# Three front attention layers taken by four streams in one round instead of two streams in two rounds

## The reference

```python
x = L0(x, ctx)   # Q = x@Wq+bq; K = ctx@Wk+bk; V = ctx@Wv+bv; x + softmax(Q K^T / 16) V @ Wo + bo
x = L1(x, ctx)   # the same Q, K, V; softmax over the QUERY axis; layernorm(x + w @ V) * gamma + beta
x = L2(x, ctx)   # as L0, with its own weights
for l in range(6):                                        # the decoder, 16 heads of 64
    tn = ln(t);  t = mha(tn, tn, ..., self_mask) + t
    tn = ln(t);  t = mha(ctx, tn, ..., ctx_mask) + t
    tn = ln(t);  t = t + relu(tn @ w1 + b1) @ w2 + b2
```

## Time and profile before

| | |
|---|---|
| median of 3 runs | 2991.25 us (2989.89 to 2992.86) |
| the profiled execution | 2991.18 us |
| its span, first to last instruction | 2989.4 us |
| TensorE matmul busy | 2846.2 us (95%) |
| VectorE, ScalarE, GpSimd busy | 1680.7, 1302.6, 963.4 us |
| mean granted TensorE clock | 0.991 |
| first matmul of the decoder | 247.99 us after the start |

### The profile page before, as it was taken

The page is one execution under the profiler, slowest core; times in us unless marked ns, Lnnn a source line. Parts: engine busy times, 40 slices in busy tenths (PEclk is TensorE's granted clock), DMA queues, the critical chain, the costliest instruction groups (busy, mean ns, idle before and its releaser), DMA issues.

```text
span 2989.4 us, 69468 instructions
## 1 busy us (share of the span) xinstructions
PE 2846.2 (95%) x23656; PEld 2311.2 (77%) x23656; DVE 1680.7 (56%) x6361; ACT 1302.6 (44%) x4274; POOL 963.4 (32%) x1169
## 2 busy tenths in 40 slices
PE   6677999999999999999999999999999999999999
PEld 4455878878878878878878878878878878878877
DVE  2344655655655655655655655655655655655655
ACT  2123444444444444444444444444444444444444
POOL 0101333333333333333333333333333333333333
PEclk9899999999999999999999999999999999999999
DMA  5003011033011032011033011032011032011010
GB/s 161 27 0 84 2 28 29 1 88 76 26 28 29 1 88 74 28 28 29 2 88 73 29 28 29 2 88 74 28 28 29 1 88 72 30 28 29 1 29 14
DMA packets 132257, 120.64 MB, mean 40 GB/s; under 512 B 15261, under 2 KB 121318, under 8 KB 130278
## 3 DMA queue, kind: packets, MB, share of 16 engines
q1 hardware_dynamic: 131942, 116.53, 15.5%
HBM read 115.59 MB, written 0.92 MB: 39 GB/s over the span
## 4 chain that ended last, share of the span: by engine, by line
issue 48%; POOL 25%; PE 21%; DVE 2%; ACT 1%; POOLq 1%; DMA 0%; SPq 0%; DVEq 0%; ACTq 0%
POOL prob L541 18%; PE proj L581 8%; PE proj L601 3%; POOL prob L511 3%; PE sum L601 3%; PE sum L769 2%; POOL ctx_parts L532 1%; PE proj L573 1%; POOL tw L491 1%; PE score L745 1%; PE tr L756 1%; DVE qcT L1197 1%; POOLq L540 1%; POOL ctx_parts L529 1%; POOL rstd L488 1%
## 5 line engine op out<-in xcount | busy, mean ns | idle before, releaser
L541 POOL TENSOR_TENSOR prob<-prob,rtotal 128x375 f32<-128x375 f32 x672 | 543.4, 812 | 762.4 <-DVE rtotal L1465 761.4
L964 ACT ACTIVATE prob<-prob,negmax 128x375 f32<-128x375 f32 (+1 forms) x688 | 418.8, 609 | 453.6 <-DVE negmax L1456 423.2
L887 PE MATMUL sum<-pT,ctx 32*128 32x224 f32 (+1 forms) x4608 | 500.6, 358 | 12.6 <-DVE qcT L1448 12.6
L887 PE MATMUL tr<-pT,ctx 32*128 32x224 f32 (+1 forms) x4608 | 500.6, 358 | 0.0
L887 PEld LDWEIGHTS sum<-pT,ctx 32*128 32x128 f32 (+1 forms) x4608 | 417.7, 185 | 73.2 <-issue 73.2
L1456 DVE CUSTOM_DVE_ANT_0 prob<-score,cbias 128x375 f32<-128x375 f32 x672 | 358.5, 533 | 195.0 <-PE score L581 193.6
L887 PEld LDWEIGHTS tr<-pT,ctx 32*128 32x128 f32 (+1 forms) x4608 | 417.0, 185 | 0.0
L581 PE MATMUL score<-ctx_parts,qc_high 128*128 128x376 f32 x1344 | 411.8, 387 | 0.0
L1474 DVE STREAM_TRANSPOSE pT<-prob 128x384 f32<-128x384 f32 x672 | 374.3, 560 | 0.0
L511 POOL TENSOR_TENSOR prob<-prob,rtotal 112x448 f32<-112x448 f32 x200 | 186.6, 933 | 543.7 <-DVE rtotal L1324 543.7
L1035 ACT ACTIVATE prob<-prob,negmax 112x112 f32<-112x112 f32 x800 | 298.9, 377 | 85.1 <-DVE negmax L1342 85.1
(11 more groups left out here) (170 smaller groups left out, 4763.2 us busy)
## 6 DMA issues: line engine op xcount, KB each, us to landing
ctx<-ctx SPq DMA_DIRECT2D x192, 176.0 KB
w_kv<-sa_kv SPq DMA_DIRECT2D x6, 2048.0 KB, 10.1
f<-ff_w SPq DMA_DIRECT2D x12, 1024.0 KB, 7.9
cmask<-ctx_mask SPq DMA_DIRECT2D x24, 375.0 KB, 4.7
w_q<-sa_q SPq DMA_DIRECT2D x6, 1024.0 KB, 11.3
w_o<-sa_ow SPq DMA_DIRECT2D x6, 1024.0 KB, 5.7
c_q<-ca_q SPq DMA_DIRECT2D x6, 1024.0 KB, 8.4
c_o<-ca_ow SPq DMA_DIRECT2D x6, 1024.0 KB, 10.8
```

What stands on the lines that cost most here:

```text
L541: pool.tensor_tensor(row, row, rtotal[:, G * SG + i:G * SG + i + 1].broadcast_to([P, S2]), ALU.mult).then_inc(prob_ready, 1)
L887: ins = pe.matmul(bank[:, 0:HT * R], ctx4[keys_of, m // (HALVES // NB), j, :], pT[keys_of, m % 2, :, j * R:(j + 1) * R], start=j == 0, sto ...
L964: act.activation(o, i, ACT.Exp, bias=negmax[0:rows, col:col + 1], scale=scale, accum_out=total[0:rows, col:col + 1]).then_inc(exp_ready, 1)
```

## The change

The front takes all four pairs in one round (`NU = PAIRS`), so its loop and the loads between rounds are gone. The order stays, with more streams in it: query and keys of stream 0, then for each stream the next query, its own scores, the next keys. The transpositions at a layer's head alternate between `proj0` and `sum0`. In the middle layer VectorE normalises stream u-1 right after the statistics of stream u. The buffers of streams 2 and 3 lie in `c_q`, `w_o`, `kT`, `before_low` and `f_1`; the context rows lie in `ctx4`, the masks in `c_o` and in the second half of `pT`, where the eighth buffer of probabilities is too. As `w_o` is borrowed, its load moves behind the front. The context masks get a semaphore of their own and are loaded later, with the self mask, behind the front's weights. Per pair, each engine has the same arithmetic instructions as before.

```diff
-    NU = 2
-    ROUNDS = PAIRS // NU
+    NU = PAIRS
+    FRONT_TR = ("proj0", "sum0")
...
+        own = (v_all, f2_flat, cq_flat, wo_flat)
+        fkT = [a[:, 0:k_end].rearrange("p (b k n) -> p b k n", b=NB, k=EK) for a in own]
+        faT = [tnT_next] + [by_chunk(kT_flat[:, u * EK * T2:(u + 1) * EK * T2]) for u in range(NU - 1)]
+        fprob = [prob_flat[:, m * S2B:(m + 1) * S2B] for m in range(NB * NU - 1)] + [pT_rest[:, 2 * NB * S2:2 * NB * S2 + S2B]]
...
 SyncE
             for u in range(NU):
-                load_pair_x(u, u)
-            load_pair_smask(0)
+                load_pair_x(u)
...
+            load_pair_smask(0)
+            for u in range(NU):
+                load_pair_fmask(u)
             load_qkv(0)
-            load_w_o(0)
             load_ca(0)
...
-            with sp.Fori(1, ROUNDS) as i:
-                for u in range(NU):
-                    sp.wait_ge(front_done, (i - 1) * NU + u + 1)
-                    load_pair_x(i * NU + u, u)
-                    load_pair_ctx(i * NU + u, u)
             sp.wait_ge(front_done, PAIRS)
+            load_w_o(0)
             load_c_q_o(0)
...
 TensorE
-            with pe.Fori(0, ROUNDS) as i:
-                pe.wait_ge(x_loaded, (i + 1) * (32 * NU))
+            pe.wait_ge(x_loaded, 16 * NU)
...
-                        transposes_of(at, ftw[u])
-                    pe.wait_ge(taken["proj0"], at.emptied("proj0", at.n["proj0"]))
+                    transposes_of(at, ftw[u], FRONT_TR[u % 2])
+                turned_to = {name: at.n[name] - NU // 2 for name in FRONT_TR}
+                def front_query(u):
+                    name = FRONT_TR[u % 2]
+                    pe.wait_ge(taken[name], at.emptied(name, turned_to[name] + u // 2 + 1))
...
-                    front_query(1)
-                    front_scores(0)
-                    front_keys(1)
-                    front_scores(1)
+                for u in range(NU):
+                    if u + 1 < NU:
+                        front_query(u + 1)
+                    front_scores(u)
+                    if u + 1 < NU:
+                        front_keys(u + 1)
...
 VectorE
+                for u in range(NU):
+                    if u + 1 < NU:
+                        front_query(u + 1)
+                    front_maxima(u)
+                    if u + 1 < NU:
+                        front_keys(u + 1)
+                    front_probabilities(u)
...
                         statistics(at, ftw[u], u)
+                        if u > 0:
+                            front_normalise(u - 1)
+                if n == 1:
+                    front_normalise(NU - 1)
             for u in range(NU):
...
+                if u == 0:
+                    dve.wait_ge(fmask_loaded, 16 * NU)
```

More of the change, by code:

```diff
@@ L257, in attention_layers @@
[L257 to L263, removed]
@@ L494, in _ @@
             pool.wait_ge(rows_loaded, 16 * ROW_DMAS)
[L495 to L504, removed]
+            at = Place(FRONT_LOOP)
+            for u in range(NU):
+                name = FRONT_TR[u % 2]
+                pool.wait_ge(ready[name], at.at(name, u // 2 + 1))
+                add_bias(fbias[0:S, 0, :], ftw[u])
+            for u in range(NU):
+                inverse_std(at, 1, u)
+            for u in range(NU):
+                name = FRONT_TR[u % 2]
+                before = {"proj0": 9 * NU - NU, "sum0": 2 * NU + NU}[name]
+                pool.wait_ge(ready[name], at.at(name, before + u // 2 + 1))
+                add_bias(fbias[0:S, 1, :], ftw[u])
             def normalise_group(at, g):
@@ L703, in _ @@
-                    if n != 1:
-                        for u in range(NU):
-                            pe.wait_ge(taken["proj0"], at.emptied("proj0", before["proj0"] + u + 1))
-                            out_rows(at, [faT[u][:, e, :] for e in range(EK)], [fwo[n][:, e, :] for e in range(EK)])
-                at.check()
+                            name = f"tr{b}"
+                            pe.wait_ge(prob_ready, at.at("prob", (n * NU + u) * NB + b + 1))
+                            bank = fill(at, name)
@@ new lines, in _ @@
+                            for j in range(KJ):
+                                ins = pe.transpose(bank[0:KR, j * S:(j + 1) * S],
+                                                   fprob[NB * u + b][0:S, j * KR:(j + 1) * KR], ident[0:S, 0:S])
+                            done(ins, name)
+                if n == 0:
+                    pe.wait_ge(ctx_loaded, 16 * NU)
+                if n == 1:
+                    pe.wait_ge(rows_loaded, 16 * ROW_DMAS)
+                for u in range(NU):
+                    for b in range(NB):
+                        if n != 1:
+                            pe.wait_ge(taken[f"tr{b}"], at.emptied(f"tr{b}", before.get(f"tr{b}", 0) + u + 1))
+                        else:
+                            pe.wait_ge(prob_ready, at.at("prob", (n * NU + u) * NB + b + 1))
+                        project(at, f"sum{b}", [fctxN[u][:, b, j, :] for j in range(KJ)],
+                                [probT[:, b, j, u * S:(u + 1) * S] for j in range(KJ)])
@@ new lines, in _ @@
+                for u in range(NU):
+                    for b in range(NB):
+                        pe.wait_ge(taken[f"sum{b}"], at.emptied(f"sum{b}", before.get(f"sum{b}", 0) + u + 1))
+                    if n != 1:
+                        for e in range(EK):
+                            project(at, f"proj{e}", [fwv[n][:, e * P:(e + 1) * P]], [fcT[u][:, :]])
+                    else:
+                        bank = fill(at, "proj1")
+                        for b in range(NB):
+                            o = bank[0:S, b * E:(b + 1) * E]
+                            pe.matmul(o, fcT[u][:, b * S:(b + 1) * S], fwv[n], start=True, stop=False)
+                            for j in range(KJ):
+                                ins = pe.matmul(o, probT[:, b, j, u * S:(u + 1) * S], fbias[0:KR, 2, :], start=False,
+                                                stop=j == KJ - 1)
+                        done(ins, "proj1")
@@ L709, in _ @@
+                if n != 1:
+                    for u in range(NU):
+                        pe.wait_ge(taken["proj0"], at.emptied("proj0", before["proj0"] + u + 1))
+                        out_rows(at, [faT[u][:, e, :] for e in range(EK)], [fwo[n][:, e, :] for e in range(EK)])
+            at.check()
             pe.wait_ge(front_done, PAIRS)
```

428 lines of the change are left out of this document (202 added, 226 removed).

## The result

The changed kernel takes 2963.88 us (median of 4 runs, 2962.96 to 2966.03) against 2992.06 (4 runs, 2989.89 to 2993.15): a ratio of 0.9907, 95% interval 0.9895 to 0.9919. That is 28.2 us less, where 31.8 was forecast; the time lies 0.6 us inside the upper end of the stated range (2964.5). Its profiled execution, whose rows follow, took 2966.03 us with a span of 2964.20 and was the slowest of the four: against the profiled execution before (2991.18) it is 25.2 us less.

A forecast was written before the change was run, and what follows sets the result against it. Only the first 247.99 us, the front, could gain; the decoder's 2741.41 us stay. Start 15.0, layers 63.6, 69.4 and 59.6, end 8.55 sum to 216.2: 31.8 us less, 2959.4, range 2955.5 to 2964.5 (chance 0.66).

The forecast's parts named there:

- (a): Layer one's head: four transpositions alternating two banks need not wait for ScalarE's copy, 4.0 us.
- (b): Layer one: the opening query, key and query fills ahead of the first scores, at the low clock, 9.03 us.
- (c): Layer one: four streams' scores, with a period of 8.0 us where a query comes between, 24.7 us.
- (d): Layer one: end of last scores to first sums, 3.35 us plus 0.95 per further stream, 5.25 us.
- (e): Layer one: first sums to first output, each further stream adding 1.35 us of sums and about 1.1 of value projection, 10.2.
- (f): Layer one: four outputs, each waiting for VectorE to empty the one bank, 2.83 us apart, 10.44 us.
- the seam: Layer two's last residual add to layer three's query: two streams still normalised, GpSimd meetings adding 1.2 us, 9.9 us.
- end of the front: Before the decoder: four pairs instead of two stored and masked behind the last add, 8.55 us, a loss of 2.35.
- (1): Rival: TensorE's clock does not fall between layers two and three; 3.0 us less, 2956.5; chance 0.12.
- (2): Rival: inserted streams in the front have a period of about 9.5 us; 9 more, 2968.5; chance 0.14.
- (3): Rival: late output weights hold the decoder's first pass, slower only beyond 83 us after request; chance 0.03 with its like.
- (4): Rival: longer load queue replaces the gap, TensorE waits 8 us or more for layer one's context rows; 2967 to 2972; 0.04.

The follow-up runs named there:

- the repeated run: The changed kernel run again without edits, beside three of the edited kernels: 2963.14 us, ratio 0.9901.
- The first experiment: The changed kernel with extra matmuls, results unread, where TensorE waits among the probability transpositions of layers one and three: 2957.06 us, ratio 0.9887.
- fillers alone: The changed kernel with unread extra matmuls at the start, in the tails, in the middle seam and before the decoder, no other edit: 2952.32 us, ratio 0.9871.
- transpositions inside: The changed kernel with each stream's probability transpositions and copies put behind the next stream's scores: 2953.67 us, ratio 0.9875.
- three edits: The changed kernel with probability transpositions behind the next stream's scores, the third layer's bias adds late and stores early: 2946.78 us, ratio 0.9853.

## Why the prediction was right, and where it was off

The mechanism was right: the gap between the rounds and the second start from cold are gone, the periods are as forecast and the decoder stays. The size is 28.2 of 31.8 us by the medians, and part of that fit is luck. In the profiled execution the decoder's first matmul comes 7.8 us later than forecast (6.1 in the profile of the repeated run, 222.29) and the gain is 25.2 us; the forecast's terms for the outer layers were too small. By its steps, in the profiled execution:

| step | forecast | measured |
|---|---|---|
| first transposition | 15.0 | 14.95 |
| layer one: transpositions (a) | 4.0 | 4.73 |
| opening (b) | 9.03 | 8.18 |
| four scores (c) | 24.7 | 24.45 |
| last scores to first sums (d) | 5.25 | 6.67 |
| first sums to first output (e) | 10.2 | 12.96 |
| four outputs (f) | 10.44 | 10.65 |
| layer two | 69.4 | 70.14 |
| of it the seam | 9.9 | 10.30 |
| layer three | 59.6 | 62.59 |
| of it the opening | 9.03 | 7.96 |
| of it last scores to first sums | 5.25 | 6.22 |
| of it sums to output | 10.2 | 13.31 |
| end of the front | 8.55 | 8.64 |
| first matmul of the decoder | 216.2 | 223.96 |
| decoder | 2741.4 | 2740.24 |

**The terms that were off** are (d) and (e), in both outer layers. In (e) I doubled the 2.70 us of 24 sums, taken at full clock, and applied the low clock only behind the holes that I had listed. The tail of transpositions doubled too, and behind it the clock fell: 2.4 and 2.8 us of the 2.8 and 3.1 that (e) misses. The first experiment gave them back. The rest of (e) is a value projection that turns in 1.25 us (67.82, 69.07), not 1.1. In (d) I read a turn as 0.93 us from the distance of two transpositions into different banks; what recurs is the turn of one bank, 1.25 us (55.51, 56.76). 3.35 + 2 x 1.25 makes 5.85, and with the clock kept the tail of layer three takes 5.83 and that of layer one 6.25, where VectorE stands 0.5 us ahead of its last division for no reason that the profile shows. The low clock adds 0.4 in each. The pieces of the turn were in the trace of before: a transposition of 0.55 (159.84), its copy of 0.51 (160.43) and 0.14 from a copy's end to the next transposition (159.70 to 159.84). I took a distance for a period.

**What held only in sum** is (a) with (b): ScalarE loads a table of 1.28 us (16.03) ahead of its first copy, so two banks do not make four transpositions back to back, and (a) is 0.7 longer; 0.85 us came back in the opening. The start's 14.95 fits 15.0, but the other kernels with the same loads have 13.7 to 14.1, so that fit is partly chance.

**Rivals.** (1) The clock kept in the seam: no; a transposition took 1.01 and the opening 7.96 us. With fillers alone it was kept, and they took 0.60 and 6.37: so this is worth 2.0 us and not 3.0. (2) Longer periods: no, 7.93 and 8.55 (91.68 to 100.23), as forecast. (3) Late output weights: the decoder changed by 1.2 us, downwards. (4) Waits for context rows: none; the chain runs from 17.93 on without a load. The four context requests did hold SyncE's queue, for 13.82 us instead of 7.99, and this was hidden as forecast.

**Two terms of the second layer.** The seam's forecast of 9.9 holds 2.3 us for meetings with GpSimd (1.2, and 1.1 within the 9.44 of before); taking them away gave 2.7, and the seam measured 10.3. The normalisation in turn, which I called hidden in 4.56 us, is: the adds stand 4.56 apart (133.31, 137.86), and the reverse order costs 4 us.

## What to carry to other kernels

When streams are added to a loop, each chain that alternates between TensorE and a copy grows with them; look for the granted clock behind such sparse stretches, not only behind holes, and put their pieces behind another stream's work, where they cost 0 to 0.3 us a layer here. That kept the clock in one layer of two; only matmuls put into the waits kept it in both. For a step that recurs, read the period of one bank, not the distance of two instructions in different banks. Work that nobody waits for yet (stores, bias adds) belongs in the slots in which its engine waits anyway: placed so, the stores gave 3.4 us and the bias adds 2.7 here.

## What the runs showed of the hardware

- The clock fell to 1.2 GHz with TensorE 0.64 busy in the microsecond before (56 to 57) and 0.98 in that of the fall; a second time at 190.4. In the kernel before TensorE was busy 0.09 and 0.65 ahead of the sums (158 to 160), and it stayed at 2.4 GHz. The Trainium skill (TensorE: Matmul & The Clock Gate, part 1) says that the throttled state is the default and that activity releases it; the traces agree in that filled tails kept the clock.
- It is not the same in each execution of the same instructions: in the version with transpositions inside, layer one's sums took 5.39 and layer three's 7.01 us; with three edits it was 7.01 and 5.39.
- Two scalings on VectorE with one tile as input (0.70 us alone) took 2.63 beside GpSimd's adds.
- ScalarE loaded a table for 1.28 us ahead of its first copy, and with it the fillers' clock was gone by the next transposition in one kernel (1.01 us) and one later in another (0.69, then 0.95).
- 1598 KB ahead of the first weights cost 4.3 to 5.6 us; four context loads held the queue that issues them 13.82 us.
